# Cross-attention and ternary feed-forward on one core: the opening's loads, layernorm and transfer order rearranged

## What is computed

```python
def xattn(query, key, value, mask):            # 16 heads of 8
    q = heads(query @ Wq + bq); k = heads(key @ Wk + bk); v = heads(value @ Wv + bv)
    scores = q @ k^T / sqrt(8)
    scores = where(mask == 0, -1e9, scores)
    return merge(softmax(scores) @ v) @ Wo + bo

def ffn(x):                                    # ternary weights, rows quantised to 8 bits
    h = gelu(bitlinear(x, w1))                 # 128 -> 512
    return bitlinear(h, w2)                    # 512 -> 128

x = x + xattn(layernorm(x), ctx, ctx, mask)
x = x + ffn(layernorm(x))
```

## Time and profile before

| | |
|---|---|
| runs | 913.99, 914.86, 914.88 us; median 914.86 us |
| profiled execution | 913.98 us, its span 912.3 us |
| mean granted TensorE clock | 0.977 |
| PE, DVE, ACT, POOL busy | 92%, 84%, 77%, 33% of the span |
| first scores with their shift (line 930) | 78.78 us |
| one pair of batches in the loop | 51.3 us (stores at 180.78 and 232.05 us) |

### The profile page before, as it was taken

How to read it: one execution, slowest core, us unless ns; L and a number is a source line. 1 busy time by engine, 2 the same in 40 slices (tenths; PEclk the granted TensorE clock), 3 DMA queues, 4 the chain that set the end, 5 groups by cost and what they waited for, 6 DMA issues and landing times.

```text
span 912.3 us, 33988 instructions
## 1 busy us (share of the span) xinstructions
PE 841.9 (92%) x11724; PEld 634.5 (70%) x11724; DVE 766.7 (84%) x2599; ACT 701.5 (77%) x1272; POOL 303.7 (33%) x360
## 2 busy tenths in 40 slices
PE   1676989999999999999999999999999999999993
PEld 1335767777777777777777777777777777777772
DVE  4887679888898989888898989888898989888954
ACT  1345768978797888979797888979797888979671
POOL 5512352323433333323433333322433333323300
PEclk9888999999999999999999999999999999999996
DMA  5433223343233333343233333343233323340100
GB/s 134 107 78 87 53 65 94 91 101 90 65 92 81 92 82 97 88 106 86 65 90 80 93 80 97 88 107 86 65 91 80 93 80 97 88 108 23 37 2 6
DMA packets 79000, 74.01 MB, mean 81 GB/s; under 512 B 10250, under 2 KB 75258, under 8 KB 78970
## 3 DMA queue, kind: packets, MB, share of 16 engines
q1 hardware_dynamic: 75695, 72.65, 31.0%
q10 hardware_dynamic: 3275, 0.97, 0.5%
HBM read 47.97 MB, written 0.92 MB: 54 GB/s over the span
## 4 chain that ended last, share of the span: by engine, by line
PE 64%; DVE 18%; issue 10%; ACT 3%; ACTq 2%; DMA 1%; DVEq 1%; SPq 1%; POOL 0%; POOLq 0%
PE ps_p L917 10%; PE ps_v L964 10%; PE ps_p L902 10%; PE ps_p L923 6%; PE ps_p L930 6%; PE ps_p L848 6%; PE ps_p L844 6%; DVE spare L1206 4%; PE ps_p L841 4%; DVE mask_bias L1113 1%; DVE row_stat L1025 1%; DVE row_stat L1026 1%; DVE row_stat L1024 1%; PE ps_p L872 1%; PE ps_p L868 1%
## 5 line engine op out<-in xcount | busy, mean ns | idle before, releaser
L1206 DVE CUSTOM_DVE_ANT_0 spare<-ps_p,mask_bias 120x500 bf16<-120x500 f32 x744 | 467.3, 673 | 49.0 <-PE ps_p L902 38.3
L737 ACT ACTIVATE probs<-ps_p 125x448 f32<-125x448 f32 x768 | 352.5, 559 | 57.1 <-PE ps_p L930 53.1
L621 POOL TENSOR_TENSOR k_lo<-k_full,keys 128x500 fp32r<-128x500 f32 x96 | 127.5, 1328 | 255.6 <-ACT keys L727 238.8
L917 PE MATMUL ps_p<-qry_lo,keys 64*125 64x448 f32 x768 | 162.8, 418 | 7.7 <-DVE seg_max L1206 2.6
L902 PE MATMUL ps_p<-keys,qry_hi 64*120 64x500 f32 x768 | 157.5, 430 | 5.6 <-DVE seg_max L1206 5.4
L964 PE MATMUL ps_v<-probs,vals 125*32 125x112 f32 x6144 | 160.7, 260 | 0.3 <-ACT probs L737 0.3
L964 PEld LDWEIGHTS ps_v<-probs,vals 125*32 125x32 f32 x6144 | 145.2, 110 | 22.4 <-issue 22.1
L923 PEld LDWEIGHTS ps_p<-qry_hi,keys 64*125 64x125 f32 x1536 | 146.0, 184 | 8.5
L930 PE MATMUL ps_p<-own_query,mask_bias 57*125 57x448 f32 x768 | 144.8, 370 | 7.5 <-DMA own_query<-shift 7.5
L923 PE MATMUL ps_p<-qry_hi,keys 64*125 64x224 f32 x1536 | 145.6, 266 | 0.0
L917 PEld LDWEIGHTS ps_p<-qry_lo,keys 64*125 64x125 f32 x768 | 72.5, 182 | 64.9 <-DVE seg_max L1206 33.0
(11 more groups left out here) (127 smaller groups left out, 885.1 us busy)
## 6 DMA issues: line engine op xcount, KB each, us to landing
keys<-k_lo SPq DMA_DIRECT2D x384, 62.5 KB, 2.0
ctx_sb<-in_ctx_dram SPq DMA_DIRECT2D x31, 750.0 KB
mask_sb<-in_mask_Bx1xSxS_ik_dram SPq DMA_DIRECT2D x64, 328.1 KB
own_query<-shift SPq DMA_DIRECT2D x64, 1.8 KB
out_dram<-x_rows SPq DMA_DIRECT2D x16, 56.0 KB, 1.6
ctx_sb<-in_ctx_dram ACTq DMA_DIRECT2D x3, 250.0 KB
x_rows<-in_x_dram SPq DMA_DIRECT2D x1, 672.0 KB, 12.7
w_sb<-in_L_ffn_w_dram SPq DMA_DIRECT2D x2, 256.0 KB, 7.2
```

The costliest lines, as they stand in the source:

```text
L621: pool.tensor_tensor(k_lo[:, (p + n) % 2, :], k_full[:, (p + n) % 2, :], keys[:, p, 0, at].bitcast(F32), ALU.subtract)\
L737: act.activation(probs[:, (c + NG * p) % NP, h], ps_p[0:KC, BANK[how]["S", c, h], 0:HC], ACT.Exp)\
L917: pe.matmul(score_bank(c, h, how), keys[rows, p, 0, at], qry_lo[rows, p, :, :], start=True, stop=False, skip_group_check=True)
L1206: dve.tensor_tensor_reduce(junk, ps_p[0:MROWS, BANK[how][slot], 0:SEG], mask_bias[0:MROWS, p, s * SEG:(s + 1) * SEG].bitcast(F32), 1.0, LO ...
```

## The change

Five things move in the opening; the loop's passes stay as they are.

1. `x` comes in one transfer (it was four tiles, then twelve), and DVE normalises all 16 tiles in one chain ahead of `open`; the slots `norm1` to `norm3` go. The normalised rows lie in a part of `probs` that is unused so early.
2. The query weights and their bias move from ACT's queue to SyncE's, behind `x`, in 8 transfers where there were 12. ACT issues the key weights ahead of the first context.
3. SyncE places the three thirds of batch 0's keys before it loads batch 1's context and mask, and not after. The loads of batch 2's mask, of the feed-forward weights and of `wo_rows` move behind the first `place_shift`; the wait for `wo_rows` on PE moves from the end of `lead` to slot `W`.
4. ACT has a one-element activation in front.
5. The slots of `open` and `lead` are written in another order on PE, ACT and DVE: `T0 T1 T2` and `K0` come ahead of `X` and `Q`, both `X0` and `X1` are in `open`, and `Q2 Q3` move into `lead`.

```diff
 PE_PASS = passes(
-    "T0 X0 T1 T2 Q0 Q1 K0 F0 K1 K2 X1 Q2 Q3",
-    "M0 M1 T0 M2 T1 X2 M3 T2 Q4 Q5 M4 K0 M5 M6 K1 M7 X3 M8 K2 Q6 Q7 M9 V0 M10 F0 V1 M11 V2 R0",
+    "T0 T1 T2 K0 X0 X1 Q0 Q1 F0 K1 K2",
+    "M0 M1 T0 M2 T1 Q2 Q3 M3 T2 X2 M4 K0 X3 M5 Q4 Q5 K1 M6 K2 Q6 Q7 M7 V0 M8 M9 V1 M10 F0 V2 M11 R0",
...
 ACT_PASS = passes(
-    "T0 X0 T1 T2 sum kf0 kh0 kf1 kh1 kf2 kh2 X1",
-    "T0 T1 X2 T2 sum kf0 kh0 kf1 kh1 X3 kf2 kh2 V0 V1 V2",
+    "T0 T1 T2 sum kf0 kh0 X0 X1 kf1 kh1 kf2 kh2",
+    "T0 T1 T2 X2 sum kf0 kh0 X3 kf1 kh1 kf2 kh2 V0 V1 V2",
...
 DVE_PASS = passes(
-    "norm1 Q0 Q1 some F0 bias0 norm2 bias1 bias2 Q2 Q3",
-    "m0 m1 norm3 m2 m3 m4 m5 Q4 Q5 m6 m7 m8 m9 m10 m11 m12 m13 some m14 m15 Q6 Q7 "
-    + " ".join(f"m{n}" for n in range(16, 20)) + " F0 m20 m21 m22 m23 neg R0 bias0 bias1 bias2",
+    "Q0 Q1 some F0 bias0 bias1 bias2",
+    "m0 m1 m2 m3 m4 m5 Q2 Q3 m6 m7 m8 m9 m10 m11 Q4 Q5 m12 m13 some m14 m15 Q6 Q7 m16 m17 "
+    + " ".join(f"m{n}" for n in range(18, 20)) + " F0 m20 m21 m22 m23 neg R0 bias0 bias1 bias2",
...
+            sp.dma_start(x_rows[:], x_groups).then_inc(x_loaded, 16)
+            for a in range(2):
+                for g in range(2):
+                    sp.dma_start(wq_sb[:, g, :]...[:, :, a, :], wq_groups[:, g]).then_inc(wq_loaded, 16)
+                for h in range(2):
+                    sp.dma_start(bq_sb[at:at + GR, :], bq_groups[h], ...).then_inc(wq_loaded, 16)
             sp.wait_ge(mask_edge[0], 2)
             load_mask(0, 0)
-            sp.dma_start(x_rows[:, 4:NT], x_groups[:, 4:NT]).then_inc(x_loaded[1], 16)
-            sp.wait_ge(ctx_loaded[0], 16)
-            sp.wait_ge(mask_edge[1], 2)
-            load(batch(0, 1))
-            sp.dma_start(wv_sb[:], wv).then_inc(wv_loaded, 16)
-            sp.dma_start(w1_sb[:], ...).then_inc(ff_loaded, 16)
-            sp.dma_start(w2_sb[:], w2).then_inc(ff_loaded, 16)
             for n in range(NSEG):
                 place_keys(batch(0, 0), n)
+            load_context(batch(0, 1))
+            sp.wait_ge(mask_edge[1], 2)
+            load_mask_of(batch(0, 1))
+            sp.dma_start(wv_sb[:], wv).then_inc(wv_loaded, 16)
...
-            load(batch(0, 2))
+            load_context(batch(0, 2))
+            for n in range(NSEG):
+                place_keys(batch(0, 1), n)
+            place_shift(batch(0, 0))
+            load_mask_of(batch(0, 2))
+            sp.dma_start(w1_sb[:], ...).then_inc(ff_loaded, 16)
+            sp.dma_start(w2_sb[:], w2).then_inc(ff_loaded, 16)
             sp.wait_ge(halves_known, 1)
...
                     sp.dma_start(wo_rows[row:row + VH, t, :], wo[at:at + VH, :]).then_inc(wo_rows_loaded, 16)
-            for n in range(NSEG):
-                place_keys(batch(0, 1), n)
-            place_shift(batch(0, 0))
...
+            act.dma_start(wk_sb[:], wk).then_inc(wk_loaded, 16)
+            act.dma_start(bk_sb[:], ...).then_inc(wk_loaded, 16)
             for n in range(NSEG):
                 act.dma_start(ctx_sb[:, 0, 4 * n:4 * n + 4], ...)
...
-            def norm_group(g):
-                dve.wait_ge(x_loaded[min(g, 1)], 16)
+            def norm_rows():
+                dve.wait_ge(x_loaded, 16)
+                statistics(chain(group_step, 0), x_rows[:], xn_stat[:], NT)
+                for t in range(NT):
+                    ins = dve.tensor_scalar(xn[:, t, :], x_rows[:, t, :], ...)
+                    if t % 4 == 3:
+                        ins.then_inc(xn_ready, 1)
```

More of the change, by code:

```diff
@@ L246, in xattn_ffn @@
         spare = sb("spare", [128, 2 * 4 * (D + PAIR)])
-        xn = spare[0:PAIR, 0:2 * 4 * D].rearrange("p (a r d) -> p a r d", a=2, d=D)
-        xn_stat = sb("xn_stat", [PAIR, 12, 4])
+        xn_stat = sb("xn_stat", [PAIR, 12, NT])
+        warm = sb("warm", [1, 1])
         xnt = spare[:, 2 * 4 * D:].rearrange("p (a n) -> p a n", a=2)
@@ L275, in xattn_ffn @@
             .rearrange("p (b k) -> p b k", b=NBANK)
+        xn = probs[:].rearrange("p n h c -> p (n h c)")[0:PAIR, NBANK * SEG:NBANK * SEG + NT * D]\
+            .rearrange("p (t d) -> p t d", d=D)
         max_junk = spare[:].bitcast(BF16)[0:MROWS, 0:NBANK * SEG].rearrange("p (b k) -> p b k", b=NBANK)
@@ L293, in xattn_ffn @@
         ps_p = es.enter_context(nc.psum_tensor("ps_p", [128, NBANK, 512], F32))
-        x_loaded = [sem("x_loaded0"), sem("x_loaded_rest")]
+        x_loaded = sem("x_loaded")
         wq_loaded = sem("wq_loaded")
@@ L428, in load_mask, with load_context, load_mask_of @@
                     sp.dma_start(mask_sb[at:at + SQ, p, :], src).then_inc(mask_loaded[p], 16)
-            def load(bt):
[L431 to L441, removed]
+            def load_context(bt):
+                b, k, p = bt
+                at, turned = b * (SK * D), NSEG * (b - 1)
+                if not isinstance(b, int):
+                    at, turned = sp.snap(at), sp.snap(turned)
+                wait(sp, ctx_t_ready, turned)
+                src = ctx_flat[bass.ds(at, SK * D)].rearrange("(c k d) -> k c d", k=KC, d=D)
+                sp.dma_start(ctx_sb[:, p], src).then_inc(ctx_loaded[p], 16)
+            def load_mask_of(bt):
+                b, k, p = bt
+                at, biased = b * (SQ * SK), NSEG * (b - 1)
+                if not isinstance(b, int):
+                    at, biased = sp.snap(at), sp.snap(biased)
+                wait(sp, mask_biased, biased)
+                load_mask(at, p)
+            def load(bt):
+                load_context(bt)
+                load_mask_of(bt)
             def place_shift(bt):
@@ L540, in _ @@
             sp.wait_ge(stored, 16 * NT)
-        N_WQ = 12
+        N_WQ = 8
         N_WO = 3
@@ L664, in _ @@
         def _(act):
+            act.dma_start(wk_sb[:], wk).then_inc(wk_loaded, 16)
+            act.dma_start(bk_sb[:], bk.rearrange("(p a) -> p a", a=1)).then_inc(wk_loaded, 16)
             ctx_0 = ctx_flat[0:SK * D].rearrange("(c k d) -> k c d", k=KC, d=D)
@@ L669, in _ @@
                     .then_inc((ctx_loaded[0], ctx_second, ctx_third)[n], 16)
[L670 to L680, removed]
             def sum_mask(bt):
@@ L760, in step @@
                         take(slot, how, bt)
+            act.wait_ge(consts, 1)
+            act.activation(warm[:], ones_f[0:1, 0:1], ACT.Copy)
             act.wait_ge(wk_loaded, 32)
@@ L805, in fill @@
                     pe.wait_ge(wtern_ready, n + 1)
+                    pe.wait_ge(wo_rows_loaded, 16 * N_WO_ROWS)
                 if kind == "V" and n == 0 and how == "lead":
@@ L855, in fill @@
                     for r in range(4):
-                        mm = pe.transpose(bank[:, r * PAIR:(r + 1) * PAIR], xn[:, n % 2, r, :], ident[0:PAIR, 0:PAIR])
+                        mm = pe.transpose(bank[:, r * PAIR:(r + 1) * PAIR], xn[:, 4 * n + r, :], ident[0:PAIR, 0:PAIR])
                 elif kind == "Q":
@@ L987, in _ @@
             step(batch(-1, 1), "lead")
-            pe.wait_ge(wo_rows_loaded, 16 * N_WO_ROWS)
             steps(pe, step)
@@ L1034, in statistics @@
                                                   in1=st[:, guess, :], op0=ALU.add, op1=ALU.mult))
-            def norm_group(g):
-                dve.wait_ge(x_loaded[min(g, 1)], 16)
[L1039 to L1044, removed]
-                ins.then_inc(xn_ready, 1)
+            def norm_rows():
+                dve.wait_ge(x_loaded, 16)
+                statistics(chain(group_step, 0), x_rows[:], xn_stat[:], NT)
+                for t in range(NT):
+                    ins = dve.tensor_scalar(xn[:, t, :], x_rows[:, t, :], xn_stat[:, 6, t:t + 1],
+                                            xn_stat[:, 11, t:t + 1], ALU.subtract, ALU.mult)
+                    if t % 4 == 3:
+                        ins.then_inc(xn_ready, 1)
             def quantise_rows(st, part):
@@ L1245, in step @@
                         quantise_hidden(st, n)
-                    elif kind == "norm":
-                        norm_group(n)
                     elif kind in TAKEN_BY_DVE:
@@ L1252, in _ @@
                 dve.memset(mask_sb[at:at + 32, 0, :], 0).then_inc(mask_edge[0], 1)
-            norm_group(0)
+            norm_rows()
             for p in range(2):
```

9 lines of the change are left out of this document (7 added, 2 removed).

## The result

| | before | changed |
|---|---|---|
| median of 7 runs each, same chip | 914.88 us (913.69 to 915.45) | 918.12 us (916.97 to 919.50) |
| profiled execution, its span | 913.98, 912.3 us | 918.12, 916.4 us |
| first scores with their shift (S) | 78.78 us | 81.83 us |

The ratio is 1.0039, with a 95% interval of 1.0027 to 1.0051: the change makes the kernel slower by 3.2 us. I had forecast 916.4, with 912.6 to 920.0 as the range, and gave "slower" and "no difference" the same chance.

A forecast was written before the change was run, and what follows sets the result against it. The opening, one chain through all engines to S, was taken as all that could change. 26.9 + 0.1 + 9.7 + 10.5 + 20.7 + 12.9 put S 2.0 us later; with 0.2 behind it, 916.4 us, range 912.6 to 920.0.

The forecast's parts named there:

- a sign of being wrong: After S: the prediction would be wrong if time was lost between the first shift and the second batch's shift.
- last third of context 0: Opening: batch 0's context fully loaded at 17.2 us, between 16.0 and 18.3, having come at 18.29 before.
- from there to `Q`: Opening: transpose, copy, sum, key work and `X0` copy, overlapping, let `Q` start 5.4 us after the context.
- two `Q`, take, flag: Opening: `Q0 Q1` 2.6 us, then DVE's second take, `some` and flag 1.7, ending batch 0's flag at 26.9.
- flag to last key placement: POOL starts 0.1 us after batch 0's flag; SyncE issues its last key placement 9.7 us later.
- context issue to T0: Batch 1's context, issued behind the key placements, takes 10.5 us to reach PE's transpose; ends 7.3 and 12.2.
- lead, T0 to flag product: From batch 1's first transpose to its flag product 20.7 us, against 23.7 before; ends 17.5 and 23.7.
- flag product to S: POOL's query and key work, twelve placements and the shift: unchanged at 12.9 us.
- behind S: Feed-forward weights and other loads issued after the shift cost 0.2 us, between 0 and 1.5.
- the first: Rival: the lead takes 23.7 us after T0, no faster than before; time 919.2, chance 0.24.
- The quick context: Rival: batch 1's context lands 7.3 us after its issue; time 912.5, chance 0.15.
- That the lead would not wait: Rival: batch 1's context is already there when T0 comes; S near 67, time 902, chance 0.03.

The follow-up runs named there:

- the kernel with the context early: The changed kernel with batch 1's context issued ahead of the twelve placements of batch 0's keys, its mask still behind them: 906.77 us, ratio 0.9912.
- the loads ahead of the shift: Batch 2's mask, feed-forward weights and `wo_rows` loaded before the first shift, against the kernel with context, mask and first shift moved early: 897.87 us, ratio 0.9816.

## Why the prediction was right, and where its sum was off

The reason held. Batch 1's context stood behind twelve key placements; PE, in order, stopped for it; S moved out by what that wait cost less what the lead gained. Undoing that order takes 11 (the context alone) to 15 us (its mask too) off; doing it alone in the kernel before adds 5.4. Most of the signs named ahead came: flag 27.70 (near 27), issue 37.69 (near 37), T0 49.38 (not before 44), maxima of DVE with a hole of 17.4 us after four, S 81.83 (80 to 82). Two went the other way: the flag product of batch 1 came 19.5 us behind T0 and not 21, and a sign of being wrong appeared, 0.83 us lost between S and the second shift.

The forecast itself stood at the line between "no difference" and "slower"; these terms moved it over:

| term | forecast | measured | difference |
|---|---|---|---|
| last third of context 0 | 17.2 | 19.05 | +1.85 |
| from there to `Q` | 5.4 | 5.27 | -0.13 |
| two `Q`, take, flag | 4.3 | 3.38 | -0.92 |
| flag to last key placement | 9.8 | 9.95 | +0.15 |
| context issue to T0 | 10.5 | 11.73 | +1.23 |
| lead, T0 to flag product | 20.7 | 19.46 | -1.24 |
| flag product to S | 12.9 | 12.99 | +0.09 |
| S | 80.8 | 81.83 | +1.03 |
| behind S | 0.2 | about 1.0 | +0.8 |

That S came within 1.0 us of the sum is partly luck: +1.85 and +1.23 stand against -0.92 and -1.24. The -0.92 also belongs to this execution: `Q0 Q1` took 1.77 us here and 3.36 in another trace with the same opening.

*The context of batch 0* was mis-sized by leaving out what the change adds beside it: the key and query weights; taking either away gave 0.4 to 1.1 us back. I had them moved at no price.

*The lead* was a sum of row lengths. Those came out as forecast (20.4 us with the flag, forecast 20.5), but neighbouring rows overlap, by 2.0 us in all, and a sum of lengths counts that twice; the one wait, 1.24 us for DVE at 66.94, was longer than my 0.2. The granted clock behind T0 was 0.50 until 54.0 and 1.00 from there on, so that `Q2 Q3` took 2.69 us, between the 3.20 and 1.67 of the earlier trace rows.

*The context of batch 1* took 11.73 us, near my upper end. Windows of the changed kernel, columns as in the earlier trace rows:

```profile
41.00:43.00 2.00, 0.00 (x0) 0.00 (x0) 0.00 (x0) 0.00 (x0) 0.00 (x0) 0.50 0.37 105
43.00:45.00 2.00, 0.00 (x0) 0.00 (x0) 0.00 (x0) 0.00 (x0) 0.00 (x0) 0.50 0.53 126
45.00:47.00 2.00, 0.00 (x0) 0.00 (x0) 0.00 (x0) 0.00 (x0) 0.00 (x0) 0.50 0.98 227
```

It moves 105 GB/s at a share of 0.37 up to 43; from there the share rises, which I read as the masks coming in beside it. What they cost shows in the kernel with the context early, where the mask is issued 18.7 us behind the context:

```profile
18.60:20.00 1.40, 1.34 (x5) 1.24 (x6) 1.29 (x4) 0.21 (x1) 0.00 (x0) 1.00 0.04 13
...
28.50:29.00 0.50, 0.32 (x1) 0.00 (x0) 0.26 (x1) 0.47 (x2) 0.44 (x1) 1.00 0.08 28
29.00:29.50 0.50, 0.00 (x0) 0.00 (x0) 0.00 (x0) 0.50 (x1) 0.50 (x1) 1.00 0.00 0
```

Issued at 18.63, that context is through between 28.5 and 29.0: 9.9 to 10.4 us, with key placements but no mask beside it. The masks account for some 1.3 to 1.8 us of the 11.7. My lower end of 7.3 was out of reach without them too: the load starts slowly (13 GB/s over its first 1.4 us), and the 0.3 us to begin had no row behind it.

The Trainium skill, DMA: Bandwidth & Descriptors, section "Anatomy of one DMA — SWDGE (gpsimd) path", has the fit of 2 us plus bytes at 436 GB/s for transfers that GpSimd issues; an estimate by it is 3.8 us for this load. SyncE issues this one, and the traces, with 9.9 to 11.7 us, are against carrying the fit over. The Trainium skill's section "Why a DMA increments its semaphore by 16 and not by 1" of the same page, by which 125 partitions go over 5 engines, fits better: 0.37 of 16 is 5.9 engines.

*The rivals.* The lead was faster than before and not as slow (19.46, decided from 21.3), so the first is false though the time came near its side. The quick context is false. That the lead would not wait is false.

*Behind S* I priced the late loads at 0.2 and named their margin as nothing. In the changed kernel they cost nothing: the feed-forward weights landed 5.4 us after their issue, near 87.5, and their reader came at 89.95, so the margin was 2.4 us. The 0.83 us lost in the first scores is the clock, which I had not in the sum there. The loads' price showed only when S came 22 us earlier: 2.35 us.

## What to carry to other kernels

A queue that is written in order is a chain: before moving a load behind work that waits for other engines, look up who reads it first and when, in the trace and not in the list; here a context and its mask, moved behind twelve placements, turned a gain of 12 us into a loss of 3. A wait costs what is not done in it, so the same order is cheap while another engine has work to catch up on and dear once that work has been moved away. And when a wait is removed, read who is late next before counting the gain: mask, key placements, shift and feed-forward weights stood behind this one in turn.

## What the runs showed of the hardware

- The granted clock in the windows reads 1.00 in the opening although the durations there are those of the lower level: in the kernel before, `Q0 Q1` take 3.33 us in a stretch that reads 1.00, and 1.67 later. Ahead of the first fall that the profile records, only durations tell the level; my "low granted clock" for the earlier trace rows rested on them.

```profile
24.00:26.00 2.00, 1.99 (x3) 1.16 (x4) 1.83 (x12) 0.30 (x2) 0.00 (x0) 1.00 1.05 240
```

- When PE first reaches its full rate differs between executions of the same opening: of the six traces with the changed kernel's instructions on PE and loads up to there, five have `Q0 Q1` at 1.77 us and one, with the loads ahead of the shift, at 3.36. That is 1.6 us on the chain. It may be one source of the spread of some 3 us among runs of one kernel; only profiled executions have a trace, so that is not shown.
- The two issues of a mask took SyncE 6.2 to 9.8 us right behind a context's issue (6.30 in the changed kernel at 38.21; 13.45 once, in the kernel before at 9.73), and 0.99 us (at 37.34, context early) when that context was 18.7 us old. In these traces the time of an issue goes with what went out just before; no run tests why.
